# Twenty token steps as a loop with straight ends, and the same steps written out in a row

## The reference, cut to what matters

```python
h = tok(x)                                   # relu(x W0) * (x W1), then Wo: 16 images of 512 tokens, 256 wide
h = concat([cls_tok, h])                     # 513 tokens
h = h + attn(layernorm(h))                   # 16 heads of 16, quantised weights and activations
h = h + ffn(layernorm(h))                    # router, best 2 of 8 experts, silu(gate) * up, down
```

## Time and profile before

| | |
|---|---|
| median of 3 runs | 2416.78 us |
| lowest and highest | 2411.87 and 2420.08 us |
| span of the profiled execution, first to last instruction | 2410.7 us |
| instructions in it | 46759 |
| TensorE busy | 2081.0 us, 86% of the span |
| VectorE busy | 1571.5 us, 65% |
| ScalarE busy | 1210.0 us, 50% |
| GpSimd busy | 911.2 us, 38% |
| mean granted TensorE clock | 0.955 |

### The profile page before, as it was taken

One profiled execution on the slowest core, in us unless ns is written; L12 is line 12 of the kernel. 1 busy time (PEld: TensorE's weight loads), 2 busy tenths in 40 slices (PEclk: granted clock), 3 DMA queues, 4 the chain that ended last, 5 costly groups with the idle time before them and its releaser, 6 DMA issues. The chain is left out here.

```text
span 2410.7 us, 46759 instructions
## 1 busy us (share of the span) xinstructions
PE 2081.0 (86%) x11964; PEld 1058.4 (44%) x12049; DVE 1571.5 (65%) x4036; ACT 1210.0 (50%) x2360; POOL 911.2 (38%) x894
## 2 busy tenths in 40 slices
PE   4889999999898898998998988861099999999997
PEld 2433444444343444443444433321066666666665
DVE  3477888887887887887888898841633333333332
ACT  1256566566565565665656666640444444444443
POOL 2222242332423423333234244133245555555554
PEclk9899999999999999999999998985599999999999
DMA  2322332322222323223232232201523333333332
GB/s 99 83 74 53 86 87 69 93 71 81 85 71 68 87 69 88 77 70 87 69 78 82 65 85 74 64 27 45 191 45 57 53 56 54 53 56 52 55 54 37
DMA packets 181071, 171.97 MB, mean 71 GB/s; under 512 B 40002, under 2 KB 169620, under 8 KB 180884
## 3 DMA queue, kind: packets, MB, share of 16 engines
q1 hardware_dynamic: 150612, 134.94, 20.1%
q0 software_dynamic: 30272, 34.80, 9.1%
HBM read 100.82 MB, written 68.93 MB: 70 GB/s over the span
## 5 line engine op out<-in xcount | busy, mean ns | idle before, releaser
L1147 DVE TENSOR_REDUCE mxs<-bank 128x1 f32<-128x512 f32 x1024 | 697.1, 685 | 205.0 <-PE bank L493 186.5
L823 ACT ACTIVATE pt<-bank 128x512 f32<-128x512 f32 x1024 | 588.5, 593 | 388.8 <-PE bank L502 369.3
L493 PE MATMUL bank<-ks,qs 96*128 96x512 bf16 x1024 | 397.9, 390 | 84.1 <-DVE mxs L1147 53.3
L502 PE MATMUL bank<-qs,ks 99*128 99x512 bf16 x1024 | 393.4, 385 | 9.2 <-ACT pt L823 8.7
L1697 POOL DMA_INDIRECT out<-y_sb,ids x136 | 214.6, 1578 | 273.3 <-DMA out<-y_sb,ids 193.7
L511 PE MATMUL bank<-pt,v_sb 128*32 128x512 f32 x2048 | 278.0, 615 | 0.0
L493 PEld LDWEIGHTS bank<-ks,qs 96*128 96x128 bf16 x1024 | 103.1, 101 | 357.5 <-DVE mxs L1147 214.0
L1826 DVE TENSOR_TENSOR hl<-bank,hh 128x512 bf16<-128x512 f32 x136 | 94.1, 692 | 210.7 <-ACT hh L1796 210.7
L1822 DVE TENSOR_TENSOR hid_e<-bank,act_g 128x512 f32<-128x512 f32 x136 | 94.1, 692 | 210.5 <-PE bank L1743 209.0
L974 POOL DMA_INDIRECT list_dram<-pay,slot_i x130 | 138.3, 1064 | 240.9 <-DVE pay L1272 206.7
L1743 PE MATMUL bank<-gu_l,xh 128*128 x544 | 206.9, 380 | 22.9 <-issue 21.2
(11 more groups left out here) (283 smaller groups left out, 3529.2 us busy)
## 6 DMA issues: line engine op xcount, KB each, us to landing
qs<-qk_dram SPq DMA_DIRECT2D x128, 128.0 KB, 2.6
ks<-qk_dram SPq DMA_DIRECT2D x64, 192.0 KB, 3.4
xt<-x_t SPq DMA_DIRECT2D x16, 512.0 KB, 4.2
h_dram<-h_sb SPq DMA_DIRECT2D x16, 512.0 KB
qs<-qk_dram SPq DMA_DIRECT2D x128, 64.0 KB, 2.2
ks<-qk_dram SPq DMA_DIRECT2D x64, 128.0 KB, 3.4
hw<-h_dram SPq DMA_DIRECT2D x16, 512.0 KB, 4.3
out<-hw SPq DMA_DIRECT2D x16, 512.0 KB, 2.9
```

The lines of the kernel that those rows point to most:

```text
L493: mm(score[u % 2][:, :], qs[0:QK, h, blk(t)], ks[0:QK, h, :], start=True, stop=True) \
L502: mm(scoret[u % 2][:, :], ks[0:QK + MROWS, h, blk(t)], qs[0:QK + MROWS, h, :], start=True, stop=True).then_inc(s("pe_st"), 1)
L823: f(pt[:, t % 2, j, :], scoret[u % 2][:, :], ACT.Exp).then_inc(s("act_exp"), 1)
L1147: v.reduce_max(mxs[:, t, g * GH + j:g * GH + j + 1], score[u % 2][:, :], AX.X).then_inc(s("dve_mx"), 1)
```

## The change

`steps` no longer makes a loop. All 20 steps are written out with constant image numbers, so that each engine's program of the token part has no loop and no register in it. The work of a step, its order and its transfers are the same.

```diff
         def fixed(i):
             body(*[At(i + o, None, 0 <= i + o < images) for o in (2, 1, 0, -1, -2)])
 
-        first = 3
-        pairs = max(0, (images - 3 - first) // 2)
-        for i in range(-2, first):
-            fixed(i)
-        if pairs:
-            with eng.Fori(0, pairs) as n:
-                for i in range(first, first + 2):
-                    body(*[At(i + o, n) for o in (2, 1, 0, -1, -2)])
-        for i in range(first + 2 * pairs, images + 2):
+        for i in range(-2, images + 2):
             fixed(i)
```

## The result

The kernel with all steps written out takes 2385.61 us (median of 4 runs, 2383.95 to 2389.34), the kernel before 2414.32 us (4 runs, 2409.41 to 2420.08; one more run than the table ahead has). The ratio is 0.9889, 95% interval 0.9868 to 0.991: 22 to 32 us faster. The prediction said 2386.2 us, 30.6 us under its base; by the medians of this comparison the gain is 2414.32 - 2385.61 = 28.7 us.

A forecast was written before the change was run, and what follows sets the result against it. A token step was taken as a chain between TensorE, VectorE's maxima and ScalarE's exponentials, leaving TensorE a few microseconds idle. Jumps 13.8 + registers 16.8 = 30.6 us off 2416.8 gave 2386.2 us; own range 2380 to 2392, whole range 2376 to 2404.

The forecast's parts named there:

- The step table: Token part, one window per step: written-out steps 2 and 13 average 93.6 us, loop steps without a jump back 95.28.
- The registers: Loop steps 3 to 12: removing register arithmetic saves 1.68 us a step, 16.8 us; TensorE's sequencer runs 7.7 a step.
- The jumps: Loop steps 4, 6, 8 and 10: removing the four jumps back on all engines saves 13.8 us.
- The clock's price: TensorE behind the first jump: granted clock 0.50, 1.2 GHz; nothing extra counted, its price being in the windows.
- The price of one branch: Loop's end: about 108 ns by the skill, making four jumps worth 0.4 us; measured durations were used instead.
- Rivals 1 and 2: Token steps: only the jumps come back, 13.8 us (chance 0.06); only the registers come back, 16.8 us (chance 0.07).
- rival 1: Steps 2 and 13 owe 1.68 us to places near the pipeline's ends; only jumps come back, 13.8 us; chance 0.06.
- Rival 3: Steps 3 to 12: straight code arrives late, some 36 packets stopping TensorE up to 1.4 us each, 2436.6 us; chance 0.04.
- Rival 4: Token steps: the registers' whole 7.7 us a step comes back, 77 + 15 us, time 2325; chance 0.03.

The follow-up runs named there:

- the far jump: Written-out kernel plus four forward jumps on TensorE, ahead of steps 5, 7, 9 and 11, each over 1200 never-run instructions: 2402.64 us.
- the near jump: Written-out kernel plus four forward jumps on TensorE, ahead of steps 5, 7, 9 and 11, each over 8 instructions: 2382.89 us.

## Why the prediction was right

**The step table.** That steps 2 and 13 already showed the written-out kernel was the step on which all rested, and it held: 93.8 to 94.2 us where the table had 93.4 and 93.8. The sum was 27.1 us in place of 30.6. The term that was off is the written-out step's length, 93.95 and not 93.6 us, ten times: step 2 doesn't wait for `qic`, and a step behind a full one does, which puts its transposition 0.62 us later. The prediction said that its figure pays for this wait, because step 13 contains it; but 93.6 is the mean of steps 13 and 2, so it paid for about half. Step 13 alone would have given 966.6 - 938 = 28.6. That the time came within 0.6 us of the forecast is partly luck: by the medians the gain is 28.7 us and not 30.6, and the kernel before came out 2.5 us lower here than the base of the forecast.

**The registers.** 16.8 us were forecast and 16.7 measured. The size came from the windows, which hold every engine's share, and so it holds; that it agrees to 0.1 us is luck, because both kinds of step are some 0.35 us longer than the prediction's (95.62 with registers where it had 95.28, 93.95 without where it had 93.6). As the cost with a share on the path it named TensorE's register instructions, 1.68 of 7.7 us a step, and there it was wrong: those cost nothing, and VectorE's cost 10.8 us in the ten. That TensorE's are hidden by products queued before was the argument for the low share; all of them are hidden. VectorE's chains of small dependent operations have no such queue ahead of them. That these are the reasons was not tried by itself.

**The jumps.** 13.8 us forecast, 10.4 by the kernel with registers and no jump; the difference is the 95.28 us that the prediction took for a step without a jump, ten times 0.34 us short. Shown by experiment: the far jump stops TensorE for 4 to 5 us, a near one for 0.2 to 0.3; TensorE's alone or VectorE's alone cost 17 us; ScalarE's, GpSimd's and SyncE's cost some 2 us at most. So they don't add: in the kernel before, TensorE and VectorE stand still over the same microseconds. That the change had to take the jumps away on both was said beforehand, and the kernel with VectorE alone in the loop bears it out by giving nothing at all. In the kernel before the jumps cost less (10.4) than TensorE's alone (17.1). One part is the `qic` wait, which a jump hides. From 455 to 1290 us it is 7.1 us with registers and no jump, and in the kernel before 3.4 us, at the four step starts of nine that are listed:

```profile
PE bank L588 <- POOL qic L1048: 3.4, 4, 0.9
```

TensorE's jumps alone hide less of it, because there is less: 2.5 us in the written-out kernel, 1.4 with its loop. That explains 3.7 - 1.1 = 2.6 of the 6.7 us; the rest, some 4 us, isn't settled. The clock's price, which the prediction left in the windows, is there: 6.2 of the 27.1 us are TensorE's busy time. So the step that said that the change can only shorten idle time was not quite right, though no product was taken away.

**The price of one branch.** The 108 ns of the Trainium skill (Advanced Engine Details and Errata, Control Flow Timing) lie between the exit's 83 ns and the near jump's 200 to 333 ns, and are far from the 4194 to 4981 ns of a far one. The far ones fit another rule of the Trainium skill (Runtime: NRT & Kernel Launch, Instruction fetch mechanics): a taken branch to code outside what an engine holds makes it wait while that code is brought. Distance and packet counts here agree with it, and so does the expert part's loop, whose branch takes 0.2 us and whose code isn't brought again.

**The rivals.** Rivals 1 and 2 gave one half of the gain each; both halves came, 10.4 and 16.7 us. Part of rival 1's reason was true all the same: step 2 owes half a microsecond, most likely to its place near the pipeline's start. Rival 3 did not appear: no idle time of issue over 0.8 us ahead of a score product in ten written-out steps. (Its 36 packets were too many, because the 86 packets of the earlier trace rows include code brought again by the jumps: with 73, the same estimate gives some 3.0 a step.) Rival 4 would have needed TensorE's 7.7 us a step, which turned out to be hidden altogether.

## What to carry to other kernels

A loop with straight ends holds its own experiment: compare a full step inside it with a full step of the same work outside it, and the window's difference is the price of jumps and registers together, before anything is built. Take for it a step whose neighbours are full too: step 2, right behind one that wasn't, was half a microsecond short. Look for that price on every engine, not on the one whose branch has a long duration: VectorE's branch took 60 ns and its jump cost as much as TensorE's of 5 us, so a loop that is taken off one of the two may give little: with TensorE's loop gone and VectorE's kept, nothing came back. Where the engine that sets the end is busy all the time and the loop's branch is cheap, as in the expert part (0.2 us), writing the loop out gave nothing.

## What the runs showed that I had not expected

- Register work on VectorE, 40 to 93 ns an instruction between operations, costs 10.8 us in ten steps; TensorE's 7.7 us a step cost nothing.
- A loop kept on VectorE alone costs the whole 27 us, 2412.82 against 2413.75 us for the kernel before in the same comparison.
- ScalarE stands still for 3.58 us behind the first jump, 12.8 us over four, and the ten steps do not lengthen by it.
- More than half of the price of TensorE's far jumps, 9.2 of 16.9 us by the profile's busy times, is products that take longer, not the standing still.
- TensorE's branch back in the expert part, over 38 us of work, takes 0.2 us; in the steps it takes 4 to 6 us.
